# Windowed attention on one Trainium2 core: the band mask is copied into PSUM by ScalarE instead of multiplied in by TensorE, with new instruction orders on every engine

## What is computed

```
q, k, v = split(shift_tokens(x) @ Wqkv)          # 16 heads of 64
q, k = rotary(l2norm(q) * qs), rotary(l2norm(k) * ksc)
sim  = q_window @ k_(previous and own window) * 8   # windows of 32 queries, 64 keys
sim  = where(key after query or more than 32 before it, -max, sim)
x    = softmax(sim) @ v @ Wo + x
xn   = layernorm(shift_tokens(x))
a, gate = split(xn @ W1 + b1);  x = (a * gelu(gate)) @ W2 + b2 + x
```

## Time and profile before

| | |
|---|---|
| time, median of 3 runs | 2398.37 us (2396.79 to 2399.0) |
| profiled execution, span from first to last instruction | 2396.9 us |
| busy share of the span: PE / DVE / ACT / POOL | 92% / 74% / 72% / 51% |
| a round of the last stage late in the run | 63.95 us |

### The profile page before, as it was taken

The page is one execution under the profiler, slowest core; times in us unless marked ns, Lnnn a source line. Parts: engine busy times, 40 slices in busy tenths (PEclk is TensorE's granted clock), DMA queues, the critical chain, the costliest instruction groups (busy, mean ns, idle before and its releaser), DMA issues.

```text
span 2396.9 us, 82108 instructions
## 1 busy us (share of the span) xinstructions
PE 2203.9 (92%) x33332; PEld 1567.5 (65%) x33332; DVE 1780.6 (74%) x3567; ACT 1719.1 (72%) x3982; POOL 1230.9 (51%) x2002
## 2 busy tenths in 40 slices
PE   6799679999976799999999999999999999999996
PEld 3487368888855566666766666666666666666662
DVE  3577377777777788888888888878888888888851
ACT  2255378888854678878888787777778888778771
POOL 0177010000001677776777776767777777767650
PEclk9899789999987899999999999999999999999997
DMA  2000021221102111112111121112111211122110
GB/s 88 10 1 1 22 98 53 80 80 53 71 2 82 30 51 51 51 47 58 51 53 42 54 72 48 45 44 60 50 41 39 75 53 51 36 64 60 40 33 22
DMA packets 40966, 117.73 MB, mean 49 GB/s; under 512 B 7952, under 2 KB 13392, under 8 KB 37776
## 3 DMA queue, kind: packets, MB, share of 16 engines
q1 hardware_dynamic: 40592, 112.49, 15.5%
HBM read 50.48 MB, written 2.23 MB: 22 GB/s over the span
## 4 chain that ended last, share of the span: by engine, by line
PE 49%; ACT 10%; issue 4%; POOL 2%; DVE 2%; DMA 1%; SPq 0%; ACTq 0%; POOLq 0%; DVEq 0%
PE w_psP L1785 12%; PE w_psT L1794 7%; PE w_psF L1729 6%; PE w_psO L1841 6%; PE w_psS L1812 5%; PE w_psF L1751 5%; PE w_psT L1823 3%; ACT w_pb L1893 3%; PE w_psF L1755 2%; PE w_psS L1803 2%; ACT w_sq L1868 1%; ACT L1893 1%; ACT L1917 1%; DMA w_xsf<-H 1%; ACT w_oT L1906 1%
## 5 line engine op out<-in xcount | busy, mean ns | idle before, releaser
L2055 POOL TENSOR_TENSOR w_ab<-w_ab,w_nrm 128x512 f32<-128x512 f32 x384 | 392.9, 1045 | 8.4 <-POOL w_nrm L84 8.4
L1893 ACT ACTIVATE w_pb<-w_psS,w_mx 128x64 f32<-128x64 f32 x1536 | 350.2, 338 | 2.8 <-DVE w_mx L1962 1.9
L2047 POOL TENSOR_TENSOR w_ab<-w_ab,w_bb 128x512 f32<-128x512 f32 x192 | 245.3, 1278 | 172.8 <-DVE w_bb L1946 171.1
L1958 DVE TENSOR_REDUCE w_nrm<-w_sq 128x8 f32<-128x512 f32 x384 | 249.5, 665 | 107.5 <-ACT w_sq L1868 107.3
L1868 ACT ACTIVATE w_sq<-w_psP 128x512 f32<-128x512 f32 x384 | 237.4, 618 | 84.7 <-DVE w_nrm L1958 42.5
L1785 PE MATMUL w_psP<-w_hi,w_xh 128*128 128x512 f32 x576 | 274.6, 477 | 25.0 <-POOL w_xl L2037 8.5
L2071 POOL TENSOR_TENSOR w_pb<-w_pb,w_sm 128x512 f32<-128x512 f32 x192 | 200.3, 1043 | 185.0 <-DVE w_sm L1971 184.5
L1794 PE MATMUL w_psT<-tables_all,w_ab 128*128 128x128 f32 x1536 | 242.0, 280 | 8.7 <-POOL w_ab L2055 4.0
L1197 DVE TENSOR_TENSOR e_glo<-e_hh,e_ghi 128x512 fp32r<-128x512 f32 x256 | 169.3, 685 | 93.0 <-ACT e_ghi L1151 92.9
L1794 PEld LDWEIGHTS w_psT<-tables_all,w_ab 128*128 128x128 f32 x1536 | 174.2, 141 | 87.3 <-ACT w_qT L1881 23.9
L1785 PE MATMUL w_psP<-w_lo,w_xh 128*128 128x512 f32 x576 | 231.1, 401 | 0.0
(11 more groups left out here) (294 smaller groups left out, 5348.5 us busy)
## 6 DMA issues: line engine op xcount, KB each, us to landing
X<-tables_layer SPq DMA_DIRECT2D x48, 384.0 KB, 3.5
X<-w_v SPq DMA_DIRECT2D x48, 384.0 KB, 3.5
e_gb<-gate_rows SPq DMA_DIRECT2D x16, 1024.0 KB, 4.7
e_raw<-in_w_moe SPq DMA_DIRECT2D x32, 256.0 KB, 5.1
w_raw<-in_w_qkv SPq DMA_DIRECT2D x20, 384.0 KB, 4.8
X<-tables_layer SPq DMA_DIRECT2D x48, 128.0 KB, 3.6
w_o<-in_w_o SPq DMA_DIRECT2D x6, 512.0 KB, 4.6
w_xs<-H SPq DMA_DIRECT2D x24, 128.0 KB, 3.3
```

What stands on the lines that cost most here:

```text
L1893: last = act.activation(pb[k % 2][:, n, :], psS[:, j, KEYS * q:KEYS * (q + 1)], ACT.Exp, bias=mx[:, n:n + 1])
L1958: dve.tensor_reduce(nrm[k // 2][:, 0, 8 * (i % 8):8 * (i % 8) + 8], sq[:, i % 2, :].rearrange("p (h d) -> p h d", d=DH), AX_X, ALU.add).th ...
L2047: pool.tensor_tensor(a, a, bb[:, i % 2, :], ALU.add).then_inc(s["ad"], 1)
L2055: pool.tensor_tensor(a, a, nrm[k // 2][:, 1, 8 * (i % 8):8 * (i % 8) + 8].unsqueeze(2).to_broadcast([128, 8, DH]), ALU.mult).then_inc(s["n ...
```

## The change

Three things change. First, the two band products at the head of every `S` are gone, but for one pair ahead of the loop. In their place ACT has a new unit `Bw k`, one instruction that copies the band (bf16, SBUF, read twice by a stride of 0) into the whole of `psS` for block k+1, once both exponentials of block k have read it. `S` now waits for that write and not for the exponentials. Second, the order table of all five engines is new. Third, nothing else: the work of the other units is the same.

```diff
                 elif kind == "S":
                     t, e = k // 2, k % 2
                     pe.wait_ge(s["te"], r * UR + 4 * t + 4)
-                    wait(pe, s["e"], r * UE + 2 * k)
-                    for h in range(2):
-                        rows = slice(64 * h, 64 * h + QB)
-                        pe.matmul(psS[:, h, 0:4 * KEYS], c.ident_bf[rows, :], c.band_bf[rows, min(k, 1), :], start=True,
-                                  stop=False, skip_group_check=True)
+                    wait(pe, s["bw"], r * NBLK + k)
...
             pe.wait_ge(s["z"], 2)
+            for h in range(2):
+                rows = slice(64 * h, 64 * h + QB)
+                pe.matmul(psS[:, h, 0:4 * KEYS], c.ident_bf[rows, :], c.band_bf[rows, 0, :], start=True, stop=False,
+                          skip_group_check=True)
             turns(pe, "pe", step)
...
+                elif kind == "Bw":
+                    act.wait_ge(s["e"], r * UE + 2 * k + 2)
+                    act.activation(psS[:, :, 0:4 * KEYS], c.band_bf[:, 0 if k == NBLK - 1 else 1, :].unsqueeze(1).to_broadcast(
+                        [128, 2, 4 * KEYS]), ACT.Copy).then_inc(s["bw"], 1)
```

Of the order tables, the lines of SP before and after, and the piece of DVE's around `xf`:

```diff
-            VE2.0-- xd0.0 VE3.0-- wd0.0- t1-- VE0.0- tl- VE1.0- xfd--""",
+            VE1.0----- VE3.0----- tl---- wd0.0--- t1----- xfd----- VE0.0---- VE2.0---- xd0.0--""",
```

More of the change, by code:

```diff
@@ L1566, in windowed_layers @@
     first = oT[:, 0:6, :].rearrange("p a b -> p (a b)")
-    names = ("wa", "wf", "wo", "tab", "scl", "z", "xst", "wd", "wh", "wl", "xh", "xl", "y", "xs", "p", "sq", "ab", "rs", "ad", "nm", "t", "te", "vx", "s", "mx", "e", "r", "pn",
+    names = ("wa", "wf", "wo", "tab", "scl", "z", "xst", "bw", "wd", "wh", "wl", "xh", "xl", "y", "xs", "p", "sq", "ab", "rs", "ad", "nm", "t", "te", "vx", "s", "mx", "e", "r", "pn",
              "pt", "pte", "av", "ot", "f", "xf", "xsf", "yn", "xn", "gg", "hh", "out")
@@ L1623, in windowed_layers @@
         "pe": """
[L1624 to L1628, removed]
@@ L1629, in windowed_layers @@
-        "act": """
[L1630 to L1636, removed]
+            P2.2- T0.2- a1--- T0.3- P2.3- Av7.0-- S0.0- g2--- V2.0- T1.0- a2--- V2.1- P3.0- T1.1- P3.1- w2---
@@ new lines, in windowed_layers @@
+            T1.2- P3.2- P3.3- T1.3- S1.0- wo0-- At0.0- V3.0- S2.0- wo1-- T2.0- V3.1- P0.0 T2.1- S3.0- T2.2- P0.1
+            At1.0- Av0.0- T2.3- P0.2 tr-- T3.0- S4.0- At2.0- P0.3 Av1.0- T3.1- V0.0 T3.2- S5.0- T3.3- V0.1 P1.0
+            At3.0- P1.1 Av2.0- P1.2 S6.0- At4.0- back-- Av3.0- At5.0- P1.3 S7.0- Av4.0- At6.0- g0-- V1.0 Av5.0-
+            V1.1 P2.0 T0.0 a0-- P2.1 At7.0- Av6.0- T0.1 g1--""",
+        "act": """
+            Te2.3-- Bw3.0-- Te3.0-- Sq0.2- Ot0.0-- Pt2.0-- Xe4.0-- Sq0.3- Xe4.1-- Te3.1-- Bw4.0-- Te3.2-- Ve0.0-
+            Te3.3-- Ot1.0-- Ve0.1- Sq1.0- Xe5.0-- Xe5.1-- Bw5.0-- Sq1.1- Pt3.0-- Sq1.2- Ot2.0-- Pt4.0-- Xe6.0--
+            Xe6.1-- Bw6.0-- Ot3.0-- Sq1.3- xn--- Pt5.0-- Xe7.0-- Ot4.0-- Pt6.0-- Xe7.1-- Ve1.0- gg0--- Ve1.1-
+            Sq2.0- Te0.0- Ot5.0-- Sq2.1- Pt7.0-- Ot6.0-- Te0.1- gg1--- Te0.2- Sq2.2- Bw7.0-- Te0.3- Sq2.3-
+            wh0.0- xh0.0 gg2--- Ve2.0- Te1.0- Ve2.1- Sq3.0- Te1.1- Sq3.1- Xe0.0- Xe0.1- Te1.2- Bw0.0- Ot7.0--
+            Sq3.2- Sq3.3- Te1.3- Xe1.0- Xe1.1- Bw1.0- Ve3.0- Pt0.0- Xe2.0- Xe2.1- Te2.0- Bw2.0- Sq0.0 Te2.1-
+            Ve3.1- Te2.2- Sq0.1 Pt1.0- Xe3.0- Xe3.1-""",
@@ L1637, in windowed_layers @@
         "dve": """
[L1638 to L1641, removed]
+            R3.1- Xd0.0- out--- R3.2- R3.3- Xm1.0- AB3.2- AB3.3- Xm2.0- xf-- Xd1.0- tb0.0 Xd2.0- AB0.0 Xm3.0-
@@ L1642, in windowed_layers @@
+            R0.0 AB0.1 R0.1 ls-- Xm4.0- AB0.2 Xd3.0- AB0.3 ln-- R0.2 Xm5.0- Xd4.0- AB1.0 R0.3 R1.0 Xd5.0- Xm6.0-
+            AB1.1 R1.1 Xd6.0- R1.2 R1.3 Xm7.0- AB1.2 AB1.3 Xd7.0- h0-- R2.0 AB2.0 AB2.1 R2.1 h1-- AB2.2 AB2.3
+            R2.2 h2-- R2.3 Xm0.0 AB3.0 AB3.1 R3.0""",
         "pool": """
-            nm2.1-- nm2.2-- Xn1.0-- ad3.2-- nm2.3-- nm3.0-- nm3.1-- Xn2.0-- ad0.0- nm3.2-- nm3.3-- lr---
-            ad0.2- Xn3.0-- Xn4.0-- ad1.0- Xn5.0-- ad1.2- Xn6.0-- Ra0.0- nm0.0- Xn7.0-- nm0.1- xl0.0
@@ L1645, in windowed_layers @@
-            nm0.2- ad2.0- nm0.3- wl0.0- ad2.2- nm1.0- nm1.1- nm1.2- nm1.3- ad3.0- Xn0.0- Ra1.0- nm2.0-""",
+            Xn3.0-- Xn4.0-- Xn5.0-- ad1.0- Xn6.0-- Ra0.0- nm0.0- Xn7.0-- ad1.2- nm0.1- nm0.2- nm0.3- ad2.0-
+            nm1.0- nm1.1- wl0.0- ad2.2- nm1.2- nm1.3- ad3.0- xl0.0 Xn0.0- Ra1.0- nm2.0- nm2.1- nm2.2- ad3.2-
+            Xn1.0- nm2.3- nm3.0- nm3.1- nm3.2- Xn2.0- ad0.0 lr-- nm3.3- ad0.2""",
         "sp": """
-            VE2.0-- xd0.0 VE3.0-- wd0.0- t1-- VE0.0- tl- VE1.0- xfd--""",
+            VE1.0----- VE3.0----- tl---- wd0.0--- t1----- xfd----- VE0.0---- VE2.0---- xd0.0--""",
```

## The result

| | before | after |
|---|---|---|
| median of 4 runs, us | 2398.7 (2396.8 to 2403.9) | 2429.3 (2428.2 to 2442.2) |
| profiled span, us | 2396.9 | 2428.3 |

The change makes the kernel slower: ratio 1.0136, 95% interval 1.011 to 1.0163. That is 36 us above the forecast and outside its range.

A forecast was written before the change was run, and what follows sets the result against it. PE was taken as nearly full everywhere (63.18 of 63.95 us), with DVE nearly as full ahead of V1.1. 2396.9 - 19 (21 rounds at 0.9) + 15 (layers' starts, net) = 2392.9, rounded 2393 us; range 2354 to 2422.

The forecast's parts named there:

- VE0 late: v's shifted copy, now issued behind `xfd`: Av0 waits 0.5 us (to 1.1) for it in normal rounds.
- Rival 2: Av0: VE0 lands later still, each 0.1 us costing 0.1 a round; 2412 us, or 2424 at 5 us landing; chance 0.22.
- 33.15: From V1.1 to the next T2.0: 34.17 us falls to 32.9, plus 0.25 for T0.0's wait for POOL.
- `tr`'s waits: In the first rounds of layers: what `tr` waits today, 3.4 us in all, goes.
- V1.1 29.9 us behind T2.0: First part of a round: DVE's list without any wait gives 29.4 us, plus 0.5 for Av0's wait; 29.78 before.
- at nothing: Bw on ACT: taken as hidden by PE work between two S; uncovered, 0.65 us a block, 5.2 a round.
- stands right on AB1.3's end: V1.1 needs the PSUM buffer AB1.3 frees: AB1.3 ends at 2078.54, V1.1 starts at 2078.61; cited against rival 1.
- Layers' first rounds: Five rounds with VE0 last in SP's queue: Av0 4.3 us late, 18 us lost, net 15 after `tr`.
- The bands' price: Band products ahead of S on PE: 0.22 us a pair, eight times a round, 1.76 us.
- Rival 4: First score products of S: they might need the bands' 0.22 us themselves; 37 us more, 2430 us; chance 0.07.
- Rival 1: PE: DVE and DMA don't hold, so a round gives back 2.2 us; 2348 us; chance 0.18.
- the forecast's own range: Whole kernel: 2378 to 2406 us, VE0 0.2 sooner to 0.4 later each round, layers' first rounds 8.4 to 10.1.

The follow-up runs named there:

- e1: The changed kernel with SP's old order, the other engines keeping the new orders: 2404.6 us, ratio 1.0007 to the kernel before.
- e5: e1 with Xd1 and tb0 ahead of xf again in DVE's list: 2401.9 us, ratio 0.9999 to the kernel before.
- e7: e1 with Xd1, tb0 and Xd2 ahead of xf in DVE's list: 2398.0 us, ratio 0.9987 to the kernel before.
- e14: The kernel before, old orders, without band products or copy (no causal mask): 2394.4 us, ratio 0.9974.
- e13: e8 without its band products, so new orders, SP's old order and no mask at all: 2387.6 us, ratio 0.9943 to the kernel before.
- e8: e1 with the band products on PE and no copy on ScalarE: 2405.6 us, ratio 1.0017 to the kernel before.
- e17: e7 with copies kept only for S0 to S4 and band products on PE for S5 to S7: 2406.3 us, ratio 1.0016 to the kernel before.
- e18: e7 with copies kept only for S0 to S2 and band products on PE for S3 to S7: 2399.1 us, ratio 0.9991 to the kernel before.
- e16: The kernel before with 16 added units of 64 products on PE ahead of Av6 of one late round: these units take 28.8 us.

## Why the prediction was wrong

- **VE0 late, right.** Forecast: issue 2.1 us behind T2.0, Av0 waits 0.5 in normal rounds, 4.3 in a layer's first. Measured: issue 2.1, Av0 later than e1's 5.21 by 0.4 to 0.5 (median), and by 3.7 on the average of the five. The price of SP's order was right too: 21 x 0.5 and 18 make 28 us, and 25 to 28 were measured. Rival 2's 2412 to 2424 came nearest to the time, but not by its reason, a VE0 that lands late in every round.
- **The gain was not there.** Against these 28 us the sum put 1.4 us a round without VE0's wait (63.95, less 29.4 and 33.15) and 3 us of `tr`'s waits, 32 us in all. e1, the change without SP's order, shows none of it: 1.0007 (0.9993 to 1.002).
- **The failed step: V1.1 29.9 us behind T2.0, by DVE's busy time with its waits set to zero and the copy "at nothing".** V1.1 stands at 32.2 in the median, with VE0's wait (the change) and without it (e1). It started from a coincidence: V1.1 "stands right on AB1.3's end" in the earlier trace rows, but no wait is listed ahead of it. It starts 0.35 us behind At6, and 0.35 or 0.36 in all 15 rounds of before, though in 7 of them AB1.3 had ended 0.2 to 1.5 us earlier. DVE did not hold V1.1 before, and e5 and e7 show that its list doesn't set it in the new orders. What the runs show in its place: PE, DVE and ScalarE are all nearly full ahead of V1.1 (13.63, 13.56 and 13.75 of 13.81 us before), and work taken off one of them turns into waits for the others. Without bands V1.1 stays at 30.5 (e14), with less on DVE's list at 32.4 (e5, e7). And the 29.78 that it was to be compared with is a short round's; the median before is 30.57, so 0.8 of the 2.3 us lies there.
- **The copy is not free.** It is hidden from S, as claimed. Yet with the copies the kernel takes 17 us more than without any mask (e1, e13), V1.1 stands at 32.2 for 31.2, and a round takes 64.30 for 63.41; with VE0 behind `xfd`, the change itself, 64.88. The forecast was 63.05.
- **Layers' first rounds, too small.** Against before they cost 20.0 us where 10.5 was forecast (15, less 0.9 in each of the five). Av0 starts 18.7 us later there than in e1, and by e1 SP's order costs 18.0, where the sum had 20.5 (five times 4.3, less 1). So the bill was not too small; the 10 us put against it didn't come, and e1 is 2.1 us slower there than before. A stretch at half clock begins within Av0's wait or just behind it in each of the five, 30.7 us in all, and nothing in the sum stood for that; but the rounds grew by no more than Av0's delay, so no run shows what the clock cost. After has 50.5 us at half clock in the 23 rounds, before 6.8, e1 31.9.
- **The 18 other rounds** lost 6.9 us where some 14 gained was forecast (16 x 0.9), and the drain 4.3 more (e1 has 4.7: it is the orders'). With the layers' 9.5 and 0.2 at the start that is 35 us, from the sum's 2392.9 to the profiled 2428.3.
- **The bands' price.** From S itself not 0.22 us goes each but 1.3 of 1.76 a round: without bands S3 takes 0.87 us to the next unit where it took 1.00, S1 and S4 0.78 and 0.79, S0 as long as before (e14). Rival 4 is out as the cause, but a quarter of its cost is real. Rival 1's premise, that a PE busy for 63.18 of 63.95 us gives back what is taken off it, is out: of 30 us PE gave back 6.
- **The range.** The lower end of the forecast's own range, 2378, doesn't follow from the terms named with it: 0.2 us in each round and 0.8 in each of the five make 2385.
- **What stays open.** In the new orders the mask costs 17 or 18 us on either engine (e1 and e8, less e13), and splitting it (e17, e18) costs no less. Why a hidden copy costs that, and what holds V1.1 at 31.2 us even in e13, no run isolates. DVE's list alone is ruled out. PE's stops are not: in rounds 2 to 22 they come to 18.8 us before, 24.0 in the change, 39.1 in e1, 21.8 in e8 and 30.8 in e13, in one traced execution of each.

## What to carry to other kernels

Before work is moved from one engine to another, leave it out and time that: here it showed 6 us to be had, not 41. An event that stands right behind another need not wait for it: look whether a wait is listed, and at more rounds than one. Read the receiving engine's load in the stretch that it will stand in, not over the round. And when a transfer is moved behind another in a queue, look at who reads it at the one place in the program where the queue is longest.

## What the runs showed of the hardware

**TensorE's instructions arrive by DMA, and dense small products outrun them.** The DMA view of e1 lists a queue of its own:

```profile
q8 instruction: 263, 4.31, 0.8%
```

That is 16 KB a packet, and between the starts of two packets PE executes 256 instructions on average (weight loads counted). All 33 stops over 0.45 us within S, At or Av of e1 end 1.2 to 1.6 us behind the end of such a packet, and in the rounds of all twenty traces no two packets start less than 3.2 us apart. In e16 256 of its small products' instructions take 1.9 us at the full clock, and PE stops after 448 and again after 256 more.

**In or behind such stops and waits the clock fell to half** (granted clock 1.00, then 0.50, the 1.2 GHz level): in e16 within the second stop, for 27.3 us, in which a unit of 0.93 us takes 1.71; in the changed kernel's first rounds of layers within Av0's wait of 2.6 to 5.6 us or just behind it, for 3.4 or 6.8 us.
